# Layer 1's neighbour gather: banded matrices, one shifting transfer per direction, the residual block added on TensorE

## The chip, the cores and the metric

The kernel is one program of four layers on one core of a Trainium2 chip, with TensorE (matrix products), VectorE (DVE), ScalarE (ACT), GpSimd (POOL) and SyncE (SP), which here only starts DMA transfers; sixteen DMA engines serve them. The metric is the device time of one execution in microseconds.

## The reference, cut to what matters

Input is 8 images of 128 channels, 64 x 64 pixels. The change touches layer 1 only. For each pixel it compares the channel vector with its nine neighbours (reflected at the borders), keeps the `kvals` most similar, averages them with exponential weights, adds a group normalisation, and puts a two-layer network behind:

```python
patches = _unfold3x3_reflect(x).reshape(B, C, K2, P)
sim = jnp.einsum('bcp,bckp->bkp', cn, pn)
order = jnp.argsort(-sim, axis=1)
mask = jnp.arange(K2)[None, :, None] < kvals
wts = jnp.exp(top_sim) * mask
wts = wts / jnp.sum(wts, axis=1, keepdims=True)
out = jnp.einsum('bckp,bkp->bcp', pat_sorted, wts).reshape(B, C, H, W)
enhanced = out + _group_norm(x, gn_weight, gn_bias)
h = jax.nn.relu(jnp.einsum('oi,bihw->bohw', w1, enhanced) + b1[None, :, None, None])
ffn = jnp.einsum('oi,bihw->bohw', w2, h) + b2[None, :, None, None]
return enhanced + ffn
```

The program adds the layer's input to this (a residual), and gathers the statistics that the next layer's normalisation needs.

## The kernel before

Images go in pairs, and `layer1` makes `PAIRS + 1` = 5 passes `t` over `STEPS` = 8 steps `c` of `ROWS` = 8 image rows. Pass t works on two things side by side: on pair t the similarities (front half), and on pair t-1 the gather and the network (back half). So pass 0 has a front half only, pass 4 a back half only. Between two passes `weights` turns the sums into weights, 43 us of small VectorE work with a few tiny transfers.

**Front half of a step.** SP loads a block of 512 pixels of both images (`xblk`, L1291). ScalarE normalises it, TensorE transposes it (L1431), and ScalarE copies it to `xt`, in which the partition is the column x of image 0 (0 to 63) or of image 1 (64 to 127) and the free axis holds rows and channels. A neighbour above is then another row in the same partition; a neighbour left or right is another partition. `shift` on SP (L1303 to L1306) makes copies moved by one column, `xleft` and `xright`: for each image and direction one transfer of 63 partitions and one of a single partition, the reflected border, eight per step. Each partition carries 9 x 128 numbers of 4 B. All of them count on the semaphore `shifted[u]`. `shift` waits first until the block is transposed and until the products of two steps before are summed (`summed`), since the copies have two slots. VectorE and GpSimd multiply `xt` with its neighbours (L1674, L1675, L1383, L1389), ScalarE squares, and VectorE sums each product over the channels into `dots` (L1681). At the end of a pass `weights` needs neighbours of `dots` and of the norms `inv_avg`; SP and ScalarE's queue fetch them by twelve small transfers each (L1362, L1619).

**Back half of a step.** TensorE starts two accumulations, one per image, with the group normalisation as a diagonal matrix (L1443). It then adds the neighbours: for each of ten source rows (`SOURCES`), `build` on VectorE (L1641) multiplies three shifted diagonals `diag` (one per dx) with the weights into `wdiag`, and `gather` (L1456) multiplies the source row, as the stationary operand, with them: one product for each dx and image. A source row reaches one, two or three target rows, so a product has 64, 128 or 192 columns. ScalarE moves the sum to `enh` (L1570); TensorE applies the network (`hidden` L1466, `down` L1472); ScalarE moves the result to `res` (L1546); GpSimd adds `enh` (L1397) and then the residual `xres` (L1399); VectorE takes statistics and SP stores. The back half of a step has four 512 KB transfers with the front half's load: `xblk`, `xsum` (for the diagonal), `xres`, and the store.

The order on each engine is written out by hand: every engine has a `step` that calls its parts in a fixed order, and all waits are on semaphores. VectorE's order in a step is builds 0 to 4, side products of the step before, builds 5 and 6, side sums, builds 7 to 9, the other sums, statistics. On SP it is the loads for the next step, `xres`, `shift`, the store of two steps before. A transposing step on TensorE stands behind the first two gathers and one hidden block.

## Time and profile before

| what | value |
|---|---|
| median of 3 runs | 5874.34 us (5872.79 to 5879.55) |
| the profiled execution's own time | 5873.65 us |
| its span, first to last instruction | 5871.9 us |
| layer 1, first block load to last statistics | about 2577 to 3573 us of the span |
| its five passes | 131.6, 174.3, 177.2, 177.8, 163.7 us |
| between the passes | about 43 us each |

The span is the time between the first and the last instruction of the profiled execution, and 1.75 us less than that execution's own time. In the rows below, positions are microseconds from the start of the span. "Busy" of an engine leaves out its register and semaphore work. Names are cut by the profile: `l_prod` is `l1_prod`, and buffer numbers are left out.

### The profile page before, as it was taken

The page shows a single profiled execution, that of the slowest core. Times are in us where ns is not written, and L with a number is a line of the kernel's source. Part 1 is how long each engine was busy: PE and PEld are TensorE (multiplying, and loading weights), DVE is VectorE, ACT ScalarE, POOL GpSimd, SP SyncE. Part 2 cuts the span into 40 slices and gives each one's busy share as a digit, 9 for nine tenths or more (in the row PEclk, how much of TensorE's full clock was granted, in tenths as well). Part 3 has the DMA queues.
Part 4 walks back from the last instruction along what each step waited for, and adds up shares of the span by engine and source line. Part 5 has one row for each costly group of instructions (what it writes and reads, how often), then busy time and mean ns, then how long its engine had stood idle before and what let it go on. Part 6 is the DMA issues. An engine that isn't in the chain of part 4 may idle for free. (4 is left out here: it accounts for less than half of the span.)

```text
span 5871.9 us, 127208 instructions
## 1 busy us (share of the span) xinstructions
PE 4826.6 (82%) x46150; PEld 3795.6 (65%) x46150; DVE 4095.5 (70%) x7785; ACT 3137.9 (53%) x5832; POOL 2837.5 (48%) x2148
## 2 busy tenths in 40 slices
PE   2887878787878787842876875999997999999996
PEld 1655555555656565622544543777777999999996
DVE  5767777776767777767987956999984555555554
ACT  1666666565656566641433424666653544456664
POOL 1535454453535454432543524888882333333364
PEclk9888989898988898965988987999998999999998
DMA  4000000000000000022433421011103000000357
GB/s 146 16 31 16 31 16 31 16 25 22 21 26 17 26 20 16 16 70 91 133 124 102 134 70 53 35 46 41 43 32 134 0 0 0 0 0 0 29 49 151
DMA packets 359128, 268.74 MB, mean 46 GB/s; under 512 B 289440, under 2 KB 290720, under 8 KB 352544
## 3 DMA queue, kind: packets, MB, share of 16 engines
q1 hardware_dynamic: 355264, 258.30, 15.4%
q8 instruction: 275, 4.51, 0.3%
q10 hardware_dynamic: 3424, 4.59, 0.2%
q14 instruction: 165, 1.35, 0.1%
HBM read 156.27 MB, written 67.11 MB: 38 GB/s over the span
## 5 line engine op out<-in xcount | busy, mean ns | idle before, releaser
L527 POOL TENSOR_TENSOR l_probs<-l_probs,l_inv 128x1024 f32<-128x1024 f32 x256 | 492.5, 1929 | 570.3 <-DVE l_inv L937 569.8
L1967 POOL TENSOR_TENSOR l_sum<-l_sum,l_prod 128x1024 f32<-128x1024 f32 x224 | 538.6, 2405 | 111.3 <-ACT l_prod L2064 92.8
L2147 DVE SCALAR_TENSOR_TENSOR l_acc<-l_xpad,l_w,l_acc 128x1024 f32<-128x1024 f32 x448 | 574.5, 1289 | 14.8 <-ACT l_acc L2048 1.3
L606 PEld LDWEIGHTS l_upper<-l_rows_T,l_hats 128*64 128x64 f32 x16384 | 516.1, 142 | 86.8 <-issue 85.0
L773 ACT ACTIVATE l_probs<-l_probs,l_shift 128x256 f32<-128x256 f32 x1024 | 506.9, 496 | 103.6 <-DVE l_shift L922 102.0
L606 PE MATMUL l_upper<-l_rows_T,l_hats 128*64 128x64 f32 x16384 | 551.4, 227 | 0.2 <-issue 0.2
L513 POOL TENSOR_TENSOR l_hats<-l_table,l_place 128x256 f32<-128x256 f32 x256 | 180.4, 705 | 765.4 <-PE l_upper L606 393.2
L590 PE MATMUL l_lower<-l_hats,l_rpe 32*128 32x256 f32 x4096 | 316.1, 425 | 262.6 <-issue 119.7
L517 POOL TENSOR_TENSOR l_hats<-l_table,l_place 128x1024 f32<-128x1024 f32 x256 | 498.7, 1948 | 0.0
L898 DVE TENSOR_SCALAR l_hats<-l_hats 128x1280 f32<-128x1280 f32 x256 | 373.2, 1458 | 168.7 <-ACT l_hats L751 168.5
L2559 DVE TENSOR_TENSOR l_sums_ps<-l_conv_odd,l_even_part 128x256 f32<-128x256 f32 x250 | 108.1, 432 | 453.4 <-PE l_conv_odd L2357 405.5
L922 DVE CUSTOM_DVE_ANT_0 l_probs<-l_lower,l_bias 128x256 f32<-128x256 f32 x1024 | 369.9, 417 | 60.3 <-PE l_lower L621 45.9
L590 PEld LDWEIGHTS l_lower<-l_hats,l_rpe 32*128 32x128 f32 x4096 | 204.3, 197 | 309.8 <-issue 222.9
L634 PEld LDWEIGHTS l_upper<-all_ident,l_probs 128*128 128x128 f32 x2048 | 259.7, 159 | 195.8 <-issue 125.5
L2487 POOL TENSOR_TENSOR l_even_lo<-l_new,l_even_hi 128x256 fp32r<-128x256 f32 x250 | 162.1, 648 | 450.8 <-DVE l_even_hi L2544 450.8
L757 ACT ACTIVATE l_rows_T<-l_lower 128x1024 f32<-128x1024 f32 x256 | 261.4, 1021 | 214.1 <-PE l_lower L590 214.1
L2357 PE MATMUL l_conv_even<-l_even_hi,l_taps 128*128 128x256 f32 x2500 | 357.9, 291 | 15.5 <-DVE l_even_hi L2544 15.2
L621 PE MATMUL l_lower<-l_keys,l_q 32*128 32x256 f32 x2048 | 344.8, 467 | 30.5 <-ACT l_bias L764 15.6
L2357 PE MATMUL l_conv_both<-l_both_hi,l_taps 128*128 128x256 f32 x2500 | 356.6, 290 | 0.0
L634 PE MATMUL l_upper<-all_ident,l_probs 128*128 128x128 f32 x2048 | 328.0, 312 | 29.4 <-POOL l_probs L527 20.9
L751 ACT ACTIVATE l_hats<-l_hats 128x1280 f32<-128x1280 f32 x256 | 323.7, 1265 | 40.2 <-POOL l_hats L517 40.2
L2357 PEld LDWEIGHTS l_conv_even<-l_even_hi,l_taps 128*128 128x128 f32 x2500 | 333.8, 192 | 16.6 <-DVE l_even_hi L2544 16.6
(325 smaller groups left out, 11891.6 us busy)
## 6 DMA issues: line engine op xcount, KB each, us to landing
l_xleft<-l_xt SPq DMA_DIRECT2D x64, 283.5 KB
l_xright<-l_xt SPq DMA_DIRECT2D x64, 283.5 KB
stat_xs<-in_x SPq DMA_DIRECT2D x8, 2048.0 KB, 23.0
l_hats<-in_x SPq DMA_DIRECT2D x8, 2048.0 KB, 7.7
l_xraw<-in_x SPq DMA_DIRECT2D x8, 2048.0 KB, 8.8
after_layer<-l_xraw SPq DMA_DIRECT2D x64, 256.0 KB, 2.0
l_xblk<-after_layer SPq DMA_DIRECT2D x32, 512.0 KB, 5.0
l_xsum<-after_layer SPq DMA_DIRECT2D x32, 512.0 KB, 5.6
```

The lines of the kernel that those rows point to most:

```text
L517: pool.tensor_tensor(xhat(ky).rearrange("c (n i) -> c n i", i=W), grid.rearrange("c (n i) -> c n i", n=1).to_broadcast([C, KW, W]), place[ ...
L527: pool.tensor_tensor(part, part, inv[:, u, cols].rearrange("c (j o) -> c j o", o=1).to_broadcast([C, 4, KEYS]), ALU.mult).then_inc(scaled_ ...
L590: last = pe.matmul(bank[r][:, h * YHAT:(h + 1) * YHAT], rpe[rows, ky // 2, GROUP_HEADS * g + h, :], yhat(ky)[rows, :], start=True, stop=True)
L606: last = pe.matmul(bank[4 + half][64 * s:64 * s + 64, n * UNITS:(n + 1) * UNITS], xhat(ky)[:, k * W:(k + 1) * W], rows_T[:, ky % 2, k, 64 ...
L621: last = pe.matmul(bank[2 * half + h][:, k * KEYS:(k + 1) * KEYS], q[rows, i * C:(i + 1) * C], keys[rows, :], start=True, stop=True)
L634: last = pe.transpose(bank[turned_bank[t]][:, m * C:(m + 1) * C], probs[:, o % 2, 4 * half + m, t * C:(t + 1) * C], sh.ident[:, :])
L773: act.activation(probs[:, u, m, :], probs[:, u, m, :], ACT.Exp, scale=-1.0, bias=shift[:, u, m:m + 1], accum_out=sums[:, u, m:m + 1]).then ...
L898: dve.tensor_scalar(slot, slot, 1.0, 0.0, ALU.subtract, ALU.min).then_inc(hats_ready, 1)
L922: last = dve.tensor_tensor_reduce(probs[:, u, m, :], bank[m // 2][:, (m % 2) * KEYS:(m % 2 + 1) * KEYS], bias[:, unit(o, m), :], 1.0, 3.0e ...
L1967: pool.tensor_tensor(part33(blk), part33(blk), rows(prod33[:, j % PRODUCTS, :]), ALU.add).then_inc(added33, 1)
L2147: last = dve.scalar_tensor_tensor(acc, src, tap, acc, op0=ALU.mult, op1=ALU.add)
L2357: last = pe.matmul(target[:, :, first:first + count], matrix(s, part, kind, j), moving[:, :, at:at + count], start=(p == 0 and q == 0), st ...
```

## The change

- **Banded matrices.** The three diagonals and their products become one band. `band` holds ones on three neighbouring diagonals, 66 columns wide; a source row and target row take 66 numbers of `wband` instead of 3 x 64. The weights are sorted by the residue of the column modulo 3 (`wres`), once per pass, by `by_residue` on VectorE: nine small operations. A gather is then one product for each source row and image, with the same 64, 128 or 192 columns: 20 instead of 60 per step.
- **One shifting transfer per direction.** `xleft[1:128]` comes from `xt` partitions 0 to 126, and `xright[0:127]` from 1 to 127: two transfers of 127 partitions a step instead of eight. The border columns now hold wrong values (a zero, or the other image's column), and the sums made of them are replaced in `dots` before the weights are made, by six two-partition transfers among the twelve on ScalarE's queue. The transfers of `inv_avg` are six instead of twelve. `xleft` and `xright` are zeroed once in the setup.
- **The enhanced block on TensorE.** `down` adds a third product to the accumulation, the identity with `enh`; GpSimd's first addition goes. ScalarE's wait before it writes `enh` again is on `ffn_in_psum` instead of `res_half`.

The diff, cut to its core:

```diff
-        diag = mem.sbuf("diag", [C, 3, W])
-        wdiag = mem.sbuf("wdiag", [C, 9 * ROWS * W])
+        THIRDS = -(-W // 3)
+        BAND = 3 * THIRDS
+        band = mem.sbuf("band", [C, BAND])
+        residue = mem.sbuf("residue", [C, 3])
+        wres = mem.sbuf("wres", [C, H + 2, 3, 3])
+        wband = mem.sbuf("wband", [C, 3 * ROWS * BAND])
...
+            is_third = smem.sbuf("is_third", [C, 3, THIRDS])
...
+                pool.memset(xleft[:, :, :, :], 0.0)
+                pool.memset(xright[:, :, :, :], 0.0)
                 pool.memset(inv_avg[:, :, :, :], 0.0)
                 pool.memset(wsrc[:, :, :, :], 0.0)
-                chain.link(pool.memset(diag[:, :, :], 0.0))
+                pool.memset(band[:, :], 1.0)
+                chain.link(pool.memset(is_third[:, :, :], 0.0))
...
+                    for sign in (-1, 1):
+                        part = band[64 * b:64 * b + 64, :]
+                        chain.link(pool.affine_select(out=part, in_=part, compare_op=ALU.is_ge, fill=0.0, base=1,
+                                                      pattern=[[sign, BAND]], channel_multiplier=-sign))
                     for k in range(3):
-                        part = diag[64 * b:64 * b + 64, k, :]
-                        chain.link(pool.affine_select(out=part, in_=part, compare_op=ALU.not_equal, fill=1.0, base=-(k - 1),
-                                                      pattern=[[-1, W]], channel_multiplier=1))
+                        part = is_third[64 * b:64 * b + 64, k, :]
+                        chain.link(pool.affine_select(out=part, in_=part, compare_op=ALU.not_equal, fill=1.0, base=-k,
+                                                      pattern=[[-3, THIRDS]], channel_multiplier=1))
...
+                dve.reduce_sum(residue[:, :], is_third[:, :, :], axis=LX)
...
-        SHIFTS = 8 * 16
-        NCOLS = 24 * 16
+        SHIFTS = 2 * 16
+        NCOLS = 18 * 16
...
-            start = sum(widths[:s]) * 3 * W
-            return wdiag[:, start:start + widths[s] * 3 * W].rearrange("p (d j x) -> p d j x", d=3, x=W)
+            start = sum(widths[:s]) * BAND
+            return wband[:, start:start + widths[s] * BAND].rearrange("p (j x) -> p j x", x=BAND)
...
-                for b in range(2):
-                    p = 64 * b
-                    sp.dma_start(xleft[p + 1:p + 64, u, :, :], src[p:p + 63]).then_inc(shifted[u], 16)
-                    sp.dma_start(xleft[p:p + 1, u, :, :], src[p + 1:p + 2]).then_inc(shifted[u], 16)
-                    sp.dma_start(xright[p:p + 63, u, :, :], src[p + 1:p + 64]).then_inc(shifted[u], 16)
-                    sp.dma_start(xright[p + 63:p + 64, u, :, :], src[p + 62:p + 63]).then_inc(shifted[u], 16)
+                sp.dma_start(xleft[1:C, u, :, :], src[0:C - 1]).then_inc(shifted[u], 16)
+                sp.dma_start(xright[0:C - 1, u, :, :], src[1:C]).then_inc(shifted[u], 16)
...
+                    at_x = lambda x: slice(x, x + W + 1, W)
+                    moves = [
+                        (inv_avg[at_x(0), 0, 0, 1:H + 1], inv_avg[at_x(1), 0, 1, 1:H + 1]),
+                        (inv_avg[at_x(W - 1), 0, 2, 1:H + 1], inv_avg[at_x(W - 2), 0, 1, 1:H + 1]),
+                    ]
+                    for p in (0, W):
+                        lo, hi = slice(p, p + W - 1), slice(p + 1, p + W)
+                        moves += [(inv_avg[hi, :, 0, 1:H + 1], inv_avg[lo, :, 1, 1:H + 1]),
+                                  (inv_avg[lo, :, 2, 1:H + 1], inv_avg[hi, :, 1, 1:H + 1])]
+                    for to, of in moves:
+                        sp.dma_start(to, of).then_inc(cols_shifted, 16)
...
-                    pool.tensor_tensor(res[:, u, b, :], res[:, u, b, :], enh[:, u, b, :], ALU.add).then_inc(res_half, 1)
-                    pool.wait_ge(res_half, g * 2 + (b + 1))
...
-                    for dx in range(3):
-                        for b in range(2):
-                            at = slice(64 * b, 64 * b + 64)
-                            last = pe.matmul(gather_ps[u][b][:, (s - 2 + first) * W:(s - 1 + final) * W], stage[at, u, s, :],
-                                             matrices(s)[at, dx, :, :].rearrange("p j x -> p (j x)"), start=False,
-                                             stop=(s == SOURCES - 1 and dx == 2))
+                    for b in range(2):
+                        at = slice(64 * b, 64 * b + 64)
+                        last = pe.matmul(gather_ps[u][b][:, (s - 2 + first) * W:(s - 1 + final) * W], stage[at, u, s, :],
+                                         matrices(s)[at, :, 0:W], start=False, stop=(s == SOURCES - 1))
...
-            def down(g, b):
+            def down(g, u, b):
                 wait(pe, ffn_copied, g * 2 + b)
                 for h in range(2):
                     pe.wait_ge(hid_ready, (g * 2 + b) * 2 + (h + 1))
-                    last = pe.matmul(ffn_ps[:, :], w2T[:, h, :], hid[:, b, h, :], start=(h == 0), stop=(h == 1))
-                last.then_inc(ffn_in_psum, 1)
+                    pe.matmul(ffn_ps[:, :], w2T[:, h, :], hid[:, b, h, :], start=(h == 0), stop=False)
+                pe.matmul(ffn_ps[:, :], sh.ident[:, :], enh[:, u, b, :], start=False, stop=True).then_inc(ffn_in_psum, 1)
...
-                wait(act, res_half, (g - 1) * 2)
+                wait(act, ffn_in_psum, (g - 1) * 2)
...
+                    moves = [
+                        (dots[at_x(0), 3, :], dots[at_x(0), 5, :]),
+                        (dots[at_x(0), 0, :], dots[at_x(0), 2, :]),
+                        (dots[at_x(0), 6, 0:H - 1], dots[at_x(1), 0, 1:H]),
+                        (dots[at_x(W - 1), 5, :], dots[at_x(W - 2), 5, :]),
+                        (dots[at_x(W - 1), 2, :], dots[at_x(W - 1), 0, :]),
+                        (dots[at_x(W - 1), 8, 0:H - 1], dots[at_x(W - 2), 2, 1:H]),
+                    ]
+                    for p in (0, W):
+                        lo, hi = slice(p, p + W - 1), slice(p + 1, p + W)
+                        moves += [(dots[hi, 3, :], dots[lo, 5, :]),
+                                  (dots[lo, 8, 0:H - 1], dots[hi, 0, 1:H]),
+                                  (dots[hi, 6, 0:H - 1], dots[lo, 2, 1:H])]
...
-                    dve.tensor_tensor(matrices(s),
-                                      diag[:, :, :].rearrange("p d (o x) -> p d o x", o=1).to_broadcast([C, 3, n, W]),
-                                      wsrc[:, first:final + 1, :, bass.ds(c * ROWS + s, 1)].rearrange("p j d o -> p d j o")
-                                      .to_broadcast([C, 3, n, W]), ALU.mult).then_inc(diag_built, 1)
+                    dve.tensor_tensor(matrices(s).rearrange("p j (m r) -> p j m r", r=3),
+                                      band[:, :].rearrange("p (o m r) -> p o m r", o=1, r=3).to_broadcast([C, n, THIRDS, 3]),
+                                      wres[:, bass.ds(c * ROWS + s, 1), first:final + 1, :].rearrange("p o j r -> p j o r")
+                                      .to_broadcast([C, n, THIRDS, 3]), ALU.mult).then_inc(diag_built, 1)
+
+            def by_residue(t):
+
+                wait(dve, diag_built, (t - 1) * STEPS * SOURCES)
+                for k in range(3):
+                    for r in range(3):
+                        d = (k + 1 - r) % 3
+                        to = wres[:, :, :, r].rearrange("p y j -> p j y")
+                        if k == 0:
+                            last = dve.tensor_scalar(to, wsrc[:, :, d, :], residue[:, k:k + 1], None, ALU.mult)
+                        else:
+                            last = dve.scalar_tensor_tensor(to, wsrc[:, :, d, :], residue[:, k:k + 1], to, op0=ALU.mult, op1=ALU.add)
+                    link(last)
...
+                    by_residue(t)
```

## Rows read from the trace of the kernel before

**Rows 1.** The page: the span, and the shortest landing of a DMA.

```profile
span 5871.9 us, 127208 instructions
...
after_layer<-l_xraw SPq DMA_DIRECT2D x64, 256.0 KB, 2.0
```

**Rows 2.** Busy time in each of the five passes of layer 1.

```profile
core 0: us, PE busy (x) PEld busy (x) DVE busy (x) ACT busy (x) POOL busy (x), PEclk, DMA share, GB/s
2577.00:2708.60 131.60, 17.80 (x64) 11.43 (x64) 91.13 (x65) 29.76 (x42) 47.25 (x16) 0.50 0.37 112
2751.70:2926.00 174.30, 155.48 (x1168) 104.86 (x1168) 158.75 (x159) 74.00 (x104) 91.52 (x44) 0.94 0.45 145
2968.70:3145.90 177.20, 159.55 (x1184) 104.69 (x1184) 163.05 (x163) 77.93 (x110) 97.85 (x48) 0.97 0.46 148
3188.70:3366.50 177.80, 160.44 (x1184) 105.36 (x1184) 162.65 (x162) 77.96 (x110) 102.46 (x48) 0.97 0.45 145
3409.30:3573.00 163.70, 158.27 (x1136) 100.11 (x1136) 73.88 (x102) 55.41 (x77) 48.41 (x36) 0.99 0.24 77
```

**Rows 3.** Time line: first shift issues of two passes, end of the first.

```profile
2585.73 0.95 SPq L1303 DMA_DIRECT2D l_xleft<-l_xt  x1
...
2696.35 2.14 DVE L1674 TENSOR_TENSOR l_prod<-l_xt,l_xleft 128x1024 f32<-128x1024 f32 x1 [1.45 <-DMA l_xright<-l_xt]
...
2708.56 0.19 DVE L1695 COPY l_dots<-l_dots 128x63 f32<-128x63 f32 x1
...
2708.80 9.51 ACTq L1619 DMA_DIRECT2D l_dots<-l_dots  x12
...
2762.58 0.82 SPq L1303 DMA_DIRECT2D l_xleft<-l_xt  x1
```

**Rows 4.** A wait inside the first pass, 2600 to 2700 us.

```profile
DVE l_prod L1674 <- DMA l_xright<-l_xt: 20.8, 4, 7.1
```

**Rows 5.** DMA packets of one step of the first pass, 2614.5 to 2626.9 us.

```profile
DMA packets 689, 1.71 MB, mean 138 GB/s; under 512 B 180, under 2 KB 180, under 8 KB 688
...
q1 hardware_dynamic: 688, 1.70, 44.4%
```

**Rows 6.** Stretches with shift transfers alone; with 2 MB loads alone.

```profile
2598.00:2602.00 4.00, 0.00 (x0) 0.00 (x0) 4.00 (x4) 0.00 (x0) 0.45 (x1) 0.50 0.56 175
2627.50:2634.50 7.00, 0.00 (x0) 0.00 (x0) 7.00 (x5) 0.00 (x0) 1.92 (x1) 0.50 0.54 161
20.00:30.00 10.00, 0.00 (x0) 0.00 (x0) 9.92 (x17) 0.00 (x0) 0.00 (x0) 1.00 1.01 431
```

**Rows 7.** A shift transfer's issue on SP, ns min/median/max.

```profile
L1303 SPq DMA_DIRECT2D l_xleft<-l_xt x64: 757/845/1410, 2585.7 to 3347.4; - x64
```

**Rows 8.** The builds on DVE, all passes, ns min/median/max.

```profile
L1641 DVE TENSOR_TENSOR l_wdiag<-l_diag,l_wsrc x320: 332/744/2908, 2752.1 to 3543.6; 128x576 f32<-128x576 f32 x96, 128x192 f32<-128x192 f32 x32, 128x384 f32<-128x384 f32 x32
```

**Rows 9.** Time line of TensorE, one step of the last pass.

```profile
3429.98 1.98 PE L1443 MATMUL l_gather_ps<-l_xsum,l_gdiag 128*128 128x512 f32 x4
3431.89 1.61 PE L1456 MATMUL l_gather_ps<-l_wdiag,l_stage 64*128 64x64 f32 x24
...
3435.35 3.19 PE L1456 MATMUL l_gather_ps<-l_wdiag,l_stage 64*128 64x192 f32 x36
...
3442.10 2.22 PE L1456 MATMUL l_gather_ps<-l_wdiag,l_stage 64*128 64x192 f32 x24
...
3446.17 2.53 PE L1456 MATMUL l_gather_ps<-l_wdiag,l_stage 64*128 64x192 f32 x36
3448.63 0.70 PE L1443 MATMUL l_gather_ps<-l_xsum,l_gdiag 128*128 128x512 f32 x1
```

**Rows 10.** Time line: a setup memset and two small forms on DVE.

```profile
2567.40 0.60 POOL L1124 MEMSET l_wsrc<- 128x594 f32 x1
...
2743.74 0.42 DVE L1760 SCALAR_TENSOR_TENSOR l_sim<-l_sim,l_edge 128x192 f32<-128x192 f32 x1
2744.19 0.35 DVE L1761 TENSOR_SCALAR l_sim<-l_sim,l_edge 128x192 f32<-128x192 f32 x1
```

More of the change, by code:

```diff
@@ L1348, in _ @@
                     sp.wait_ge(cols_ready, t + 1)
-                    for b in range(2):
-                        p = 64 * b
-                        lo, hi = slice(p, p + 63), slice(p + 1, p + 64)
-                        first, second, but1, last = (slice(p + q, p + q + 1) for q in (0, 1, 62, 63))
-                        moves = [
-                            (inv_avg[hi, 0, 0, 1:H + 1], inv_avg[lo, 0, 1, 1:H + 1]),
-                            (inv_avg[hi, 1, 0, 1:H + 1], inv_avg[lo, 1, 1, 1:H + 1]),
-                            (inv_avg[lo, 0, 2, 1:H + 1], inv_avg[hi, 0, 1, 1:H + 1]),
-                            (inv_avg[lo, 1, 2, 1:H + 1], inv_avg[hi, 1, 1, 1:H + 1]),
-                            (inv_avg[first, 0, 0, 1:H + 1], inv_avg[second, 0, 1, 1:H + 1]),
-                            (inv_avg[last, 0, 2, 1:H + 1], inv_avg[but1, 0, 1, 1:H + 1]),
-                        ]
-                        for to, of in moves:
-                            sp.dma_start(to, of).then_inc(cols_shifted, 16)
+                    at_x = lambda x: slice(x, x + W + 1, W)
[9 more added lines that the diff above has]
+                        sp.dma_start(to, of).then_inc(cols_shifted, 16)
                     sp.wait_ge(weights_ready, t + 1)
@@ L1488, in step @@
                     if before:
-                        down(g, 0)
+                        down(g, 1 - u, 0)
                         hidden(g, 1 - u, 1)
@@ L1493, in step @@
                     if before:
-                        down(g, 1)
+                        down(g, 1 - u, 1)
                     if t >= 1:
@@ L1507, in _ @@
                 hidden(g, 1, b)
-                down(g, b)
+                down(g, 1, b)
         @block.scalar
@@ L1605, in _ @@
                     act.wait_ge(summed, (t + 1) * STEPS)
-                    for b in range(2):
-                        p = 64 * b
-                        lo, hi = slice(p, p + 63), slice(p + 1, p + 64)
-                        first, second, but1, last = (slice(p + q, p + q + 1) for q in (0, 1, 62, 63))
-                        moves = [
-                            (dots[hi, 3, :], dots[lo, 5, :]),
-                            (dots[first, 3, :], dots[first, 5, :]),
-                            (dots[lo, 8, 0:H - 1], dots[hi, 0, 1:H]),
-                            (dots[last, 8, 0:H - 1], dots[but1, 2, 1:H]),
-                            (dots[hi, 6, 0:H - 1], dots[lo, 2, 1:H]),
-                            (dots[first, 6, 0:H - 1], dots[second, 0, 1:H]),
-                        ]
-                        for to, of in moves:
-                            act.dma_start(to, of).then_inc(cols_shifted, 16)
+                    at_x = lambda x: slice(x, x + W + 1, W)
+                    moves = [
[11 more added lines that the diff above has]
+                                  (dots[hi, 6, 0:H - 1], dots[lo, 2, 1:H])]
+                    for to, of in moves:
+                        act.dma_start(to, of).then_inc(cols_shifted, 16)
                     act.wait_ge(sims_ready, t + 1)
```

2 lines of the change are left out of this document (removed).

## The prediction

> **What bounds the kernel now.** The change lies in layer 1 alone, so I read the page for the span, 5871.9 us [rows 1], then busy time by pass. Layer 1 makes five passes over eight steps each: pass 0 computes neighbour sums only, passes 1 to 3 those of one pair of images and the output of the pair before, pass 4 output only. They last 131.6, 174.3, 177.2, 177.8 and 163.7 us [rows 2], with some 43 us of weight arithmetic after each of the first four. What limits them differs. In passes 1 to 3 VectorE is busy 159 of 174 us and TensorE 155, both nearly full. In pass 4 TensorE is busy 158 of 164. In pass 0 neither is: VectorE 91 of 131.6, with TensorE at its 1.2 GHz level (granted 0.50) [rows 2]. The wait view says what VectorE lacks there: in 100 us it idles 20.8 us before the first side product, for the right shifting transfer [rows 4]. So SBUF-to-SBUF transfers already end last in pass 0, with eight transfers a step in place. That sent me to the DMA views.
>
> **How those transfers run.** One step of pass 0 issues four transfers of 63 rows, four of one row and one 512 KB load. The queue counts 688 packets, 180 of them under 512 B [rows 5]. A row is 4608 B (9 x 128 x 4). Four times 63 rows are 252 packets; a single row went as 16 packets of 288 B, so 64; the load is 256 packets of 2 KB. That leaves 116 tiny ones, and 116 = 4 x 9 + 5 x 16: one completion from each of nine engines for a 63-row transfer, from each of sixteen for the others. With sixteen everywhere the sum would be 716 and 208. The share agrees: while shifts run alone, 0.56 and 0.54 of the sixteen engines are busy [rows 6], and 9/16 is 0.5625. So a transfer's rows are not dealt out freely: 63 rows = 9 engines x 7, 128 rows = 16 x 8. Both are what comes out if the engine count is the largest number up to 16 that divides the rows.
>
> **The shifting transfers of the change.** Per direction there is now one transfer of 127 rows. 127 is prime. By the pattern just read the count is 1, and 585,216 B go through one engine; two directions make 1.170 MB a step. The trace has no one-engine transfer of this size, so its pace is bounded by two rows. Below: nine engines with the same packets move 161 GB/s at share 0.54, 161/(0.54 x 16) = 18.6 GB/s each [rows 6]. Above: sixteen engines with whole-image loads move 431 GB/s, 26.9 each [rows 6]. I take 25.5, near the upper row, since the nine read and write the same half of the partitions at the same time and a lone engine has no such company. That is 1.170 MB / 25.5 GB/s = 45.9 us a step (43.5 to 62.9), against a whole step now of about 131.6/8 = 16 us in pass 0 and 176/8 = 22 us in passes 1 to 3.
>
> The same engine also carries its sixteenth of each 512 KB transfer, 32.8 KB or 1.3 us: one in a step of pass 0, four (block, sum and residual loads, store) in passes 1 to 3. Both directions must share an engine for this sum; had they two, it is the second rival. A step then takes S0 = 45.9 + 1.3 = 47.2 us (44.7 to 64.7) in pass 0 and S1 = 45.9 + 5.2 = 51.1 us (48.4 to 69.9) in passes 1 to 3.
>
> The Trainium skill says the same outright, and names this very case: in "DMA: Bandwidth & Descriptors", section "Why a DMA increments its semaphore by 16 and not by 1", a DMA issued from SP or ACT uses the largest count up to 16 that divides the slowest dimension of both patterns, 127 partitions get 1, and it is always the lowest-numbered engines that are taken. The completions counted above bear out the rule at 63 and 128 rows; no row here shows it at 127, nor which engine is taken. By its last part both directions queue on one engine. Its rule for authors (one transfer rather than two halves) speaks for the change, this rule against it, and by this rule the sum is the one above.
>
> **Does the engine stay busy?** Shift c is issued by SP once step c is turned and the products of step c-2 are summed. Those products wait for shift c-2. From its landing VectorE needs about 12.2 us (2696.35 to 2708.56) [rows 3], and the turn behind TensorE's first gathers and hidden block about 10 us more at the low clock. Meanwhile shift c-1 runs for 47 us or more. So the next is always queued in time, the engine never idles, and steps cost exactly S. The same slack hides everything else in passes 0 to 3, where compute needs 22 us of a 47 to 51 us step. SP is in order: behind a late shift wait the store of step c-2 and the next block, sum and residual loads, all of them needed one step later only.
>
> **Sum of the passes.** Pass 0: first issue to last column now takes 2708.56 - 2585.73 = 122.8 us [rows 3]; then 8 x 47.2 + 2.0 (a landing, [rows 1]) + 12.2 = 391.8, so +269. Passes 1 to 3: first issue 10.9 us after the pass begins (2751.7 to 2762.58) [rows 2, 3], about 2 us more with the new vector step below, then 8 x 51.1 + 2.0 + 12.2: 435.9 each, 1307.7 in all against 529.3 now [rows 2], so +778.
>
> **Builds.** 10 a step; one of 192, 384 or 576 elements takes 332 to 744 ns undisturbed (median 744 for the widest) [rows 8], so 0.126 us plus 1.07 ns an element. With 66, 132 and 198 elements they cost 2 x 0.20 + 2 x 0.27 + 6 x 0.34 = 3.0 us in place of 6.2. In passes 1 to 3 this is worth nothing: the transfer covers it. Without that cover it is in the first rival.
>
> **Gathers and identity.** A TensorE step of pass 4 runs from 3429.98 to 3448.63, 18.65 us; its gathers take 1.61 + 3.19 + 2.22 + 2.53 = 9.55 us [rows 9]. Two in three go: -6.4. The identity adds one 128x512 product per image; a group of two products takes 1.98 us with its tail, about 0.86 each [rows 9]: +1.7. So -4.7 a step, -37 us in pass 4, nothing in passes 1 to 3. If ScalarE's hand-overs end last instead, a part stays away: -20 to -37, I take -37. POOL loses one of two additions; it is on no path except the last microseconds.
>
> **New work by residue.** Nine VectorE forms of 198 elements ahead of each of passes 1 to 4: like 0.35 and 0.42 us for 192 elements [rows 10], 3 x 0.35 + 6 x 0.42 = 3.6 us, on the path. For passes 1 to 3 it is in the 2 us above (quicker first builds give back 1.6); pass 4 +3.6.
>
> **Setup.** Two memsets of 2304 elements; 594 elements took 0.60 us [rows 10], so 2 x 2.3 or less, say 4, and 1 for four selects: +5 (0 if weight loads hide it).
>
> **Edges.** inv_avg goes by 6 transfers, not 12, dots still by 12 on ACT's queue, and that chain, 9.51 us of issues [rows 3], ends last: 0 (-4 to +1 over all four).
>
> Total: 5873.65 (the profiled execution's own time; its span is 5871.9 and the median of the runs 5874.34, so no correction) + 269 + 778 - 37 + 4 + 5 = **6893 us**. At 26.9 GB/s the steps lose 2.5 x 8 + 2.7 x 24 = 85 us: 6808. At 18.6 they gain 17.5 x 8 + 18.8 x 24 = 591: 7484.
>
> **Rivals.** (1) *Faster: the rows are dealt out unevenly over most engines.* If 127 rows go as eight to an engine, transfers end no later than now and SP issues two instead of eight (0.85 us the larger, [rows 7]). Then TensorE sets passes 1 to 3, 155.5/8 = 19.4 - 4.7 = 14.7 us a step, VectorE with POOL beside it about as much; say 15.5 against 20.8: -127 us over 24 steps. Pass 4 gives -37, pass 0 about -15 of its waits, new work +19: 5714 us (5690 to 5790). It decides from the point where a shift transfer lands within some 15 us; for that 127 rows must get five engines or more. Against it: 63 rows would then have got more than nine.
> (2) *Two engines.* Each direction gets one engine, but not the same. The step falls by half of 45.9: 6893 - 32 x 22.95 = 6159 us. Against it: nothing shows transfers of one queue taking turns among engines, but nothing excludes it either.
> (3) *Nothing moves:* gains and a partly slower transfer cancel. It needs a pace in a narrow band.
>
> **Chances.** Forecast 0.87, rival 1 0.08, rival 2 0.04, rival 3 0.01. Range 6800 to 7490: the forecast's own, with both ends of the pace; it leaves out 0.13. A run of this kernel can tell a difference of about 0.2%, 12 us. Faster 0.08, same 0.01, slower 0.91.
>
> **What the profile after would show.** DMA share near 1/16 = 0.06 through pass 0, at 23 to 27 GB/s; steps of 47 and 51 us; VectorE waiting 30 us a step on xleft or xright; TensorE at its low level in passes 0 to 3; a packet count of 254 rows a step with 2 completions; pass 4 near 130 us. Wrong if the share stays above 0.3 in pass 0 (rival 1), or is 0.12 (rival 2). Steps of 60 us and more would mean the pace was mis-sized, gaps in the DMA row between steps that SP's waits are late.

## The result, and the profile after

The changed kernel takes **6848.09 us** (median of four runs, 6846.43 to 6849.19) beside 5874.9 us for the kernel before on the same chip: ratio 1.1655 with a 95% interval of 1.1635 to 1.1675. It is slower by a sixth, in the way that was forecast; the forecast was 6893 us, the range 6800 to 7490.

The page, its span line, its busy line, and the group of the first side product (busy us, mean ns, then the idle time of VectorE just before it and what ended most of it).

```profile
span 6845.7 us, 122063 instructions
...
PE 4785.2 (70%) x43718; PEld 3675.8 (54%) x43718; DVE 4004.6 (58%) x7822; ACT 3130.8 (46%) x5832; POOL 2721.0 (40%) x2091
...
L1690 DVE TENSOR_TENSOR l_prod<-l_xt,l_xleft 128x1024 f32<-128x1024 f32 x32 | 83.6, 2612 | 1137.6 <-DMA l_xright<-l_xt 922.8
```

VectorE idles 1137.6 us in all ahead of 32 side products. In the kernel before it was 72.2 us, so this wait alone grew by 1065 us, more than the loss of 973 us (6848 - 5875):

```profile
L1674 DVE TENSOR_TENSOR l_prod<-l_xt,l_xleft 128x1024 f32<-128x1024 f32 x32 | 51.6, 1613 | 72.2 <-DMA l_xright<-l_xt 61.0 <-issue 10.4 <-DVE l_dots L1681 0.5
```

The busy times by pass (columns as in [rows 2], which they answer):

```profile
2579.00:2967.20 388.20, 17.80 (x64) 11.43 (x64) 90.11 (x65) 29.76 (x42) 40.73 (x16) 0.50 0.10 38
3012.90:3432.30 419.40, 150.49 (x556) 77.86 (x556) 133.92 (x159) 72.35 (x104) 65.84 (x30) 0.64 0.16 57
3477.20:3900.20 423.00, 159.12 (x576) 79.95 (x576) 137.67 (x162) 75.80 (x110) 68.28 (x32) 0.66 0.17 58
3945.20:4367.00 421.80, 155.83 (x576) 78.43 (x576) 137.32 (x163) 75.78 (x110) 68.28 (x32) 0.67 0.16 57
4411.90:4545.40 133.50, 129.32 (x532) 62.05 (x532) 42.19 (x102) 54.63 (x77) 23.55 (x18) 0.98 0.27 85
```

Pass 0 went from 131.6 to 388.2 us, passes 1 to 3 from some 176 to some 421, with none of the compute engines busy for even half of them; pass 4, which has no shifting transfers, fell from 163.7 to 133.5. The DMA view of one step of pass 0, 2636.5 to 2682 us (40 slices, GB/s in each), against [rows 5, 6]:

```profile
DMA  0000000000000000000000000003930000000000
GB/s 25 28 24 28 24 28 28 24 28 24 28 24 28 24 28 24 28 24 28 24 28 24 28 28 24 28 24 75 312 118 28 24 28 24 28 24 28 28 24 25
DMA packets 524, 1.69 MB, mean 37 GB/s; under 512 B 18, under 2 KB 18, under 8 KB 524
...
l_xblk<-after_layer SPq DMA_DIRECT2D x1, 512.0 KB, 37.5
```

The GB/s row never falls below 24 and never rises above 28 but for the one 512 KB load in the middle: one engine, always busy. 18 small packets are 16 completions of that load and one for each direction's shift. A step of pass 2, 3587.1 to 3637.9 us, has no gap either, and four transfers of 512 KB in it:

```profile
GB/s 26 26 26 27 25 25 29 25 25 25 29 38 25 29 25 25 29 25 25 25 29 25 25 29 25 25 25 103 330 33 176 255 53 278 121 148 278 33 25 26
```

The time line of VectorE in pass 0, and of SP's issues in a step of pass 1:

```profile
2636.28 3.39 DVE L1690 TENSOR_TENSOR l_prod<-l_xt,l_xleft 128x1024 f32<-128x1024 f32 x1 [57.26 <-DMA l_xright<-l_xt]
...
2682.22 3.33 DVE L1690 TENSOR_TENSOR l_prod<-l_xt,l_xleft 128x1024 f32<-128x1024 f32 x1 [34.65 <-DMA l_xright<-l_xt]
```

```profile
3166.15 15.38 SPq L1314 DMA_DIRECT2D l_xright<-l_xt  x1
3181.57 22.04 SPq L1333 DMA_DIRECT2D after_layer<-l_res  x1
3203.73 2.66 SPq L1303 DMA_DIRECT2D l_xblk<-after_layer  x1
3206.44 3.29 SPq L1328 DMA_DIRECT2D l_xsum<-after_layer  x1
3209.77 0.47 SPq L1321 DMA_DIRECT2D l_xres<-after_layer  x1
3210.35 7.17 SPq L1313 DMA_DIRECT2D l_xleft<-l_xt  x1
3217.56 15.75 SPq L1314 DMA_DIRECT2D l_xright<-l_xt  x1
```

A step of pass 0 is 45.9 us (2682.22 - 2636.28), one of passes 1 to 3 is 50.8. The issues are the surprise: an issue of a shift took 0.8 to 1.4 us before [rows 7], and now 15 us for the right shift and 22 for the store. The likely reading is that the queue to the one engine is full and the sequencer stands in the issue until there is room; no view shows the queue itself.

### The profile page after: what moved, and what is told of

Same layout as the page of the kernel before. It is cut to its first block and busy times, and to the rows that moved or that the text cites. A ratio compares the mean times of both kernels' runs of the same rounds, so it can differ in the third digit from the quotient of the medians.

```text
span 6845.7 us, 122063 instructions
## 1 busy us (share of the span) xinstructions
PE 4785.2 (70%) x43718; PEld 3675.8 (54%) x43718; DVE 4004.6 (58%) x7822; ACT 3130.8 (46%) x5832; POOL 2721.0 (40%) x2091
## 5 line engine op out<-in xcount | busy, mean ns | idle before, releaser
L1690 DVE TENSOR_TENSOR l_prod<-l_xt,l_xleft 128x1024 f32<-128x1024 f32 x32 | 83.6, 2612 | 1137.6 <-DMA l_xright<-l_xt 922.8
L1458 PE MATMUL l_gather_ps<-l_wband,l_stage 64*128 64x192 f32 (+2 forms) x1280 | 150.7, 371 | 631.4 <-DVE l_wband L1644 631.4
L606 PEld LDWEIGHTS l_upper<-l_rows_T,l_hats 128*64 128x64 f32 x16384 | 515.7, 142 | 86.5 <-issue 84.7
L1394 POOL TENSOR_TENSOR l_prod<-l_xt,l_xright 128x1024 f32<-128x1024 f32 x32 | 86.5, 2704 | 1094.6 <-DMA l_xright<-l_xt 1094.6
L1458 PEld LDWEIGHTS l_gather_ps<-l_wband,l_stage 64*128 64x128 f32 x1280 | 114.9, 220 | 722.0 <-DVE l_wband L1644 664.9
L1547 ACT ACTIVATE l_res<-l_ffn_ps,l_b 128x512 f32<-128x512 f32 x64 | 44.0, 687 | 861.8 <-DMA after_layer<-l_res 538.8
L2374 PE MATMUL l_conv_even<-l_even_hi,l_taps 128*128 128x256 f32 x2500 | 357.4, 290 | 15.7 <-DVE l_even_hi L2561 15.4
```

Of the source, the lines that this page charges most:

```text
L606: last = pe.matmul(bank[4 + half][64 * s:64 * s + 64, n * UNITS:(n + 1) * UNITS], xhat(ky)[:, k * W:(k + 1) * W], rows_T[:, ky % 2, k, 64 ...
L1458: last = pe.matmul(gather_ps[u][b][:, (s - 2 + first) * W:(s - 1 + final) * W], stage[at, u, s, :], matrices(s)[at, :, 0:W], start=False, ...
L2374: last = pe.matmul(target[:, :, first:first + count], matrix(s, part, kind, j), moving[:, :, at:at + count], start=(p == 0 and q == 0), st ...
```

## The experiments

Unless told otherwise each is timed against the kernel before on the same chip; a step is the distance between two starts of the first side product, a pass runs from the scaled identity (gdiag) to the last column.

**Was it the transfers alone?** The changed kernel with the eight old transfers:

```
-                sp.dma_start(xleft[1:C, u, :, :], src[0:C - 1]).then_inc(shifted[u], 16)
-                sp.dma_start(xright[0:C - 1, u, :, :], src[1:C]).then_inc(shifted[u], 16)
+                for b in range(2):
+                    p = 64 * b
+                    sp.dma_start(xleft[p + 1:p + 64, u, :, :], src[p:p + 63]).then_inc(shifted[u], 16)
+                    sp.dma_start(xleft[p:p + 1, u, :, :], src[p + 1:p + 2]).then_inc(shifted[u], 16)
...
-        SHIFTS = 2 * 16
+        SHIFTS = 8 * 16
```

> The changed kernel with the old eight shifting transfers of a step (63 rows and 1 row for each image and direction); banded matrices, edge mending, identity and the rest stay. Theory (one engine carries all 127 rows of both directions): all of the loss goes and the rest of the change shows its own worth, about 5720 us (5690 to 5790), DMA share in pass 0 back near 0.37. Rival (the slowdown comes from another part: the builds or gathers waiting, the mended edges, the identity): stays above 5875 us, near 6848.

Measured: 5790.41 us, ratio 0.9854 (0.9837 to 0.9870). So two lines of the change make 1058 us of loss (6848 - 5790), and the rest of it is a gain of some 86. That gain is less than was expected of it (5720 us): passes 1 to 3 come down to 148, 159 and 156 us, where eight steps of 15.5 us would be 124.

**What sets the number of engines?** The same kernel with each direction in two parts, once 112 + 15 rows, once 125 + 2 (there the pairs are 0, 125 and 125, 127):

```
+                for lo, hi in ((0, 112), (112, 127)):
+                    sp.dma_start(xleft[lo + 1:hi + 1, u, :, :], src[lo:hi]).then_inc(shifted[u], 16)
+                    sp.dma_start(xright[lo:hi, u, :, :], src[lo + 1:hi + 1]).then_inc(shifted[u], 16)
```

> The changed kernel with each direction cut in two: 112 rows and 15 rows, four transfers a step; both numbers have a divisor of 14 to 16. Theory (the count of engines is the largest number up to 16 that divides the rows): 16 and 15 engines, so at most 8 rows of a direction on one engine, no limit left, 5700 us (5670 to 5780), at or a little below the kernel with eight transfers since SP issues half as many. Rival (a transfer that spans both images' halves, or more than 64 partitions, or the shared semaphore, is what is slow): 112 rows span both halves too, so it stays near 6848.

> Each direction as 125 rows and 2 rows. Theory: 125 rows go on 5 engines, 25 rows each; the fullest engine carries about 52 rows a step, 52 x 0.175 = 9.1 us and up to 5 us of the other loads, 14 us: just under the step that compute sets, so 5720 to 5800 us with a DMA share near 5/16 while shifts run. Rival (rows are dealt unevenly, or the count has nothing to do with divisors): 125 and 127 rows differ by 2 per cent, near 6830.

Measured: 5750.23 us (0.9786, 0.9769 to 0.9802) with 112 + 15, and 5839.09 us (0.9938, 0.9921 to 0.9955) with 125 + 2. Same bytes, same number of transfers, 89 us apart. A stretch of pass 0 with nothing but rows of the 125 + 2 transfers in flight (columns as in [rows 2]: the last two are DMA share and GB/s), one with nothing but those of 112 + 15, and two landings of the latter:

```profile
2622.00:2624.00 2.00, 0.00 (x0) 0.00 (x0) 2.00 (x2) 0.00 (x0) 0.00 (x0) 0.50 0.32 92
...
2617.00:2619.00 2.00, 0.00 (x0) 0.00 (x0) 2.00 (x3) 0.00 (x0) 0.00 (x0) 0.50 0.98 267
```

```profile
l_xleft<-l_xt SPq DMA_DIRECT2D x1, 504.0 KB, 4.0
l_xright<-l_xt SPq DMA_DIRECT2D x1, 504.0 KB, 4.8
```

0.32 of sixteen is five engines, and 5 is the largest divisor of 125 up to 16. 112 = 16 x 7 goes over all, a share of 0.98: such a transfer lands in 4 to 5 us, where a 127-row pair takes 44. The share of 9/16 for 63 rows [rows 6] and of 1/16 for 127 are the other two points of the same pattern. The Trainium skill, "DMA: Bandwidth & Descriptors", section "Why a DMA increments its semaphore by 16 and not by 1", states this as its rule, and the runs agree at 63, 112, 125 and 127 rows.

**Do both directions really queue on one engine?** First one direction alone in one piece, the other as before (four transfers):

```
                 sp.dma_start(xleft[1:C, u, :, :], src[0:C - 1]).then_inc(shifted[u], 16)
-                sp.dma_start(xright[0:C - 1, u, :, :], src[1:C]).then_inc(shifted[u], 16)
+                for b in range(2):
+                    p = 64 * b
+                    sp.dma_start(xright[p:p + 63, u, :, :], src[p + 1:p + 64]).then_inc(shifted[u], 16)
+                    sp.dma_start(xright[p + 63:p + 64, u, :, :], src[p + 62:p + 63]).then_inc(shifted[u], 16)
```

> Left as one transfer of 127 rows, right as the old four. Theory (both directions queue on the same engine): the one engine carries 127 rows instead of 254, and the nine-engine transfers add 14 to it, 141 x 0.175 = 24.7 us; steps of 26 us in pass 0 and 30 us in passes 1 to 3 instead of 45.7 and 49.6, so 6848 - 8 x 20 - 24 x 20 = 6210 us (6150 to 6300). Rival (the two directions were on two engines side by side, each at half the pace): one direction alone still takes its 45 us, near 6848.

Measured: 6234.21 us (one run). Steps are 26 to 27 us in pass 0 and 30 to 32 after it: of the 254 rows of a step the engine still carries 127 and one in nine of the 126 that go in 63-row transfers, so 141, and a step of pass 0 falls from 45.8 to some 27 us. One direction alone doesn't take its old 45 us.

Then the right shift moved to ScalarE's queue, right behind its copies of the turned block, where the old wait for the summed products is met:

```
-                sp.dma_start(xright[0:C - 1, u, :, :], src[1:C]).then_inc(shifted[u], 16)
...
+                        act.wait_ge(turn_copied, (n + 1) * 2)
...
+                        act.dma_start(xright[0:C - 1, u, :, :], rows_of(t, c * ROWS, ROWS + 1)[1:C]).then_inc(shifted[u], 16)
```

> The changed kernel, but the right shifting transfer (127 rows) is issued by ScalarE's queue, right behind the turned copies, the left one still by SP's. Theory A (every one-engine transfer goes to the same engine, whatever queue issues it): steps stay 45.8 and 50.8 us, DMA share 0.06, 6848 us (6820 to 6900). Theory B (each queue deals from an engine of its own): two engines at once, steps near 24 and 28 us, DMA share 0.12, 6848 - 32 x 22.9 = 6115 us (6080 to 6200).

Measured: 6834.29 us (one run), theory A. With nothing but the two queues' shifts in flight:

```profile
2600.00:2630.00 30.00, 0.00 (x0) 0.00 (x0) 0.00 (x0) 0.00 (x0) 0.00 (x0) 0.50 0.06 26
...
2597.23 18.16 SPq L1313 DMA_DIRECT2D l_xleft<-l_xt  x1
2597.23 0.65 ACTq L1595 DMA_DIRECT2D l_xright<-l_xt  x1
...
2615.84 42.08 SPq L1303 DMA_DIRECT2D l_xblk<-after_layer  x1
```

A share of 0.06 and 26 GB/s from two queues is still one engine. A second queue doesn't bring a second engine; SP waits even longer, 42 us, in the issue of a load. ScalarE doesn't: its issue at 2597.23 us, to the same engine and at the same moment as one of SP's that takes 18.16 us, is over in 0.65, and the median of its 32 is 0.65 too (9.3 the longest). So what is held up is the queue that has the backlog, and not every issuer.

**Two engines.** Cut at 122 = 2 x 61:

```
+                for lo, hi in ((0, 122), (122, 127)):
```

> The changed kernel with each direction cut into 122 and 5 rows. If the engine count is the largest number up to 16 that divides the rows, 122 rows (2 x 61) go over two engines and 5 rows over five: the two busiest engines carry 61 + 1 rows of each direction, a step of (2 x 62 x 4608 B)/26.4 GB/s = 21.6 us and 1.3 more in pass 0, 5.2 in passes 1 to 3: 23 and 27 us. Then 6848 - 32 x 23.5 = 6096 us (6060 to 6150). If rows were dealt by size or evenly: 5750 as with 112 rows.

Measured: 6140.93 us (one run), 45 us above the estimate but nowhere near the 5750 of 112 rows. The share with shifts alone is that of two engines:

```profile
2604.00:2608.00 4.00, 0.00 (x0) 0.00 (x0) 0.00 (x0) 0.00 (x0) 0.00 (x0) 0.50 0.13 53
```

Steps are 23.4 us in pass 0 (23 expected) and 29.0 in the middle of passes 1 to 3 (27 expected). Of the 2 us, some 1.6 are a term that was mis-sized (4 x 0.4, next section); the rest isn't explained.

**Does the engine hide all the rest?** The kernel before with only the transfers of the change, its moves of dots and inv_avg and its two memsets; diag, wdiag, three products a source and POOL's two additions stay:

```
+                sp.dma_start(xleft[1:C, u, :, :], src[0:C - 1]).then_inc(shifted[u], 16)
+                sp.dma_start(xright[0:C - 1, u, :, :], src[1:C]).then_inc(shifted[u], 16)
```

> The kernel before, with only the two 127-row transfers (and the edges mended in the dots); three products per gather, wide matrices and POOL's two additions stay. Theory (in passes 0 to 3 the one DMA engine sets the step and hides all compute): steps of 45.8 and 50.8 us as in the changed kernel, so the same time but for pass 4, which stays at some 164 us from its scale (+30), and without the four by_residue of 4.05 us (-16): 6862 us (6845 to 6885). Rival (the longer builds and gathers still count behind a late transfer): a step longer by some of the 3.2 us of builds, up to +77 us more, 6900 to 6940.

Measured: 6861.01 us, ratio 1.1678 (1.1658 to 1.1697). Its middle steps, 45.6 to 45.9 and 50.4 to 51.2 us, are those of the changed kernel although TensorE makes three times the gather products and VectorE's builds are longer. In passes 1 to 3 those parts are worth nothing beside this transfer (1263 us in all against 1264). Its pass 2, then pass 4 (as in [rows 2]; 423.0 and 133.5 us in the changed kernel):

```profile
3465.20:3888.20 423.00, 180.09 (x1184) 119.53 (x1184) 169.26 (x163) 76.81 (x110) 93.01 (x48) 0.72 0.17 62
4392.10:4556.60 164.50, 159.09 (x1136) 100.56 (x1136) 73.92 (x102) 55.43 (x77) 48.44 (x36) 0.98 0.24 77
```

**What are the other parts worth?** Each alone on the kernel before. The bands (with by_residue), then the identity, then the transfers cut at 112:

```
-                    for dx in range(3):
-                        for b in range(2):
...
+                    for b in range(2):
...
+                                         matrices(s)[at, :, 0:W], start=False, stop=(s == SOURCES - 1))
```

> The kernel before, with only the banded matrices (one product per source and image, by_residue); eight shifting transfers, POOL's two additions. If the gain of the eight-transfer run (0.985) is the gathers' 6.4 us a step on TensorE and the builds' 3.2 on VectorE, it is nearly all here or more, since the identity costs TensorE 1.7 us a step: pass 4 -40, passes 1 to 3 -60, by_residue +16: 5785 us (5765 to 5810). Rival (the second addition on POOL is what holds VectorE and ScalarE's hand-overs, so the gathers' saving is not used without the identity): 5830 or more.

```
-                    pool.tensor_tensor(res[:, u, b, :], res[:, u, b, :], enh[:, u, b, :], ALU.add).then_inc(res_half, 1)
+                pe.matmul(ffn_ps[:, :], sh.ident[:, :], enh[:, u, b, :], start=False, stop=True).then_inc(ffn_in_psum, 1)
```

> The kernel before, with only the enhanced block added by TensorE's identity. Theory (TensorE is near full in passes 1 to 4, and two more products a step lie on it): +1.7 us a step in pass 4 (+14), passes 1 to 3 0 to +1.7 a step: 5895 us (5875 to 5930), slower. Rival (POOL's addition held up VectorE or the block's end): faster, 5840 to 5870.

```
-                for b in range(2):
...
+                for lo, hi in ((0, 112), (112, 127)):
```

> The kernel before, with only the shifts as four transfers of 112 and 15 rows over 16 and 15 engines and mended edges. Theory (in passes 1 to 3 compute sets 21 us of the step, the transfers only part of its waits): pass 0 -12, passes 1 to 3 -10, setup +5: 5857 us (5835 to 5875). Rival (transfers over nine engines already set the steps of passes 1 to 3 of the kernel before): -25 or more from passes 1 to 3 as between the two runs with bands and identity, 5830 or less.

Measured: bands 5796.35 us (0.9863, 0.9847 to 0.9880); identity 5919.87 us (1.0070, 1.0053 to 1.0087); transfers 5841.21 us (0.9940, 0.9923 to 0.9956). Pass 2 of the three, then pass 4 of bands alone, of bands with identity (the run with eight transfers), and of identity alone:

```profile
2958.10:3121.00 162.90, 124.10 (x544) 62.96 (x544) 134.36 (x162) 76.90 (x110) 84.70 (x48) 0.89 0.47 152
...
2975.40:3168.10 192.70, 176.28 (x1216) 112.58 (x1216) 151.67 (x163) 77.94 (x110) 74.00 (x32) 0.96 0.43 136
...
2946.90:3120.60 173.70, 159.43 (x1184) 104.67 (x1184) 159.73 (x163) 77.97 (x110) 107.07 (x48) 0.98 0.48 151
...
3376.50:3495.00 118.50, 112.94 (x496) 54.60 (x496) 49.45 (x103) 54.68 (x77) 46.85 (x36) 0.98 0.30 96
...
3355.40:3489.20 133.80, 129.60 (x532) 62.07 (x532) 42.21 (x102) 54.64 (x77) 23.54 (x18) 0.98 0.26 85
...
3446.20:3624.10 177.90, 173.70 (x1172) 106.94 (x1172) 65.30 (x102) 55.42 (x77) 22.84 (x18) 0.99 0.22 71
```

The bands give 82 us, nearly all of the gain. The identity alone **costs** 42 us: TensorE is nearly full in the kernel before, as VectorE is, and in pass 2 it is now busy 176 us against 160 [rows 2]. On top of the bands it neither gains nor loses (0.9863 and 0.9854, with intervals that overlap; the run with both also has the mended edges, some 7 us less, and the two memsets, some 4 more), but not evenly: passes 1 to 3 last 463 us in all with it and 481 without, while pass 4, where POOL has no products to make and its additions are free, is 133.8 us with it and 118.5 without. The cut at 112 rows is worth 37 us by itself and 40 on top of the other two; most of it falls in pass 0 (106.8 us from the first shift to the last column, against 122.8) and 11 us in passes 1 to 3, so transfers over nine engines didn't set the steps there. On top of the other two, where the steps are shorter, passes 1 to 3 get 26 of the 40 us (463 to 437).

**A version that beats both.** With 112 + 15 rows; the scaled identities before the wait for the shifted weights, and POOL's two memsets moved from ahead of its masks to behind them:

```
+                pool.sem_inc(masks_ready, 1)
+                pool.memset(xleft[:, :, :, :], 0.0)
+                pool.memset(xright[:, :, :, :], 0.0)
...
+                    scales(t)
+                    dve.wait_ge(weights_shifted, WS * t)
+                    by_residue(t)
```

> The version with 112 and 15 rows (5750 us), with the scaled identities built before the wait for the shifted weights and by_residue behind them, and POOL's two memsets of the shifted buffers issued after its masks, where they hold up nobody. If by_residue and the memsets lie on the path: four times 4 us and 4.6 us less, 5730 us (5722 to 5740). Rival (VectorE's first builds of a pass wait for by_residue anyway and the pass starts with them): only the memsets, 5746.

Measured: 5738.02 us (0.9767, 0.9751 to 0.9783): 12 us of the 20. Setup is shorter by 2.1 us only: the first block load is issued 12.4 us after the layer's first transfer, 14.5 with the memsets ahead and 9.9 in the kernel before, so moving them gives back half of that 4.6 us. The rest is theirs too, for the most part: the run with bands and no memsets has 10.6, those with the new transfers and memsets but no bands 13.4. Why they still cost behind the masks isn't shown. And from the last vector form of the weights to the first side product of pass 2 the gain is 1.8 us, not 4. What became of the rest is in TensorE's rows around the start of that pass, first in this version, then in the one with 112 + 15 alone (windows as in [rows 2], where the value ahead of the last two is the granted clock, then the first gathers and the hidden block's products):

```profile
2914.00:2918.00 4.00, 3.75 (x4) 1.17 (x4) 0.00 (x0) 0.00 (x0) 0.00 (x0) 0.50 0.24 50
2918.00:2922.90 4.90, 0.00 (x0) 0.00 (x0) 4.34 (x11) 0.00 (x0) 0.00 (x0) 0.50 0.93 321
...
2922.98 1.23 PE L1459 MATMUL l_gather_ps<-l_wband,l_stage 64*128 64x64 f32 x8 [5.15 <-DVE l_wband L1645]
2924.14 3.40 PE L1468 MATMUL l_hid_ps<-l_enh,l_w1T 128*128 128x512 f32 x4
```

```profile
2931.40:2934.00 2.60, 2.60 (x14) 1.45 (x14) 0.53 (x2) 0.69 (x1) 0.00 (x0) 1.00 0.00 0
...
2931.43 0.72 PE L1459 MATMUL l_gather_ps<-l_wband,l_stage 64*128 64x64 f32 x8
2932.07 1.98 PE L1468 MATMUL l_hid_ps<-l_enh,l_w1T 128*128 128x512 f32 x4
```

Last, the same with the blocks of the last pair of images added by POOL, those of the first three by the identity:

```
+                if not last_pair:
+                    last = pe.matmul(ffn_ps[:, :], sh.ident[:, :], enh[:, u, b, :], start=False, stop=True)
...
+                    if last_pair:
+                        pool.tensor_tensor(res[:, u, b, :], res[:, u, b, :], enh[:, u, b, :], ALU.add).then_inc(res_half, 1)
```

> The version with 112 and 15 rows and the earlier scales (5738 us), but the blocks of the last pair are added by GpSimd as in the kernel before, those of the first three pairs by TensorE's identity. From the traces: with bands alone pass 4 takes 118.5 us from its scale to its last statistic, with bands and identity 133.8; in passes 1 to 3 the identity saves some 18 us in all. If the identity's cost in pass 4 is TensorE's (GpSimd has no products there): -15 us, 5723 us (5717 to 5730). Rival (the saving of the run with bands alone is its shorter hand-overs in another order, or the tail's second addition takes it back): 5735 or more.

Measured: **5725.63 us** (0.9742, 0.9729 to 0.9755), 12 us less again, all of it in pass 4, which takes 127.7 us from its scales where the version ahead took 139.9. This is 152 us better than the kernel before and 1122 better than the change.

## Why the prediction was right, step by step

**The engine count** held: 127 rows on one engine, both directions on the same. It came from the packets and shares of 63 rows [rows 5, 6], and the runs with 112, 122, 125 and 127 rows show it (shares 0.98, 0.13, 0.32 and 0.06).

**The pace** was a choice, 25.5 GB/s between 18.6 and 26.9. A step of passes 1 to 3 is 50.8 - 45.8 = 5.0 us longer than one of pass 0 and moves three more 512 KB transfers: by this subtraction 1.7 us for each one's sixteenth, where 1.3 was reckoned. That leaves 45.8 - 1.7 = 44.1 us for 1.170 MB, 26.5 GB/s. The upper row was the right neighbour. The trace doesn't show why a load costs 1.7 us: 32.8 KB in that time would be 20 GB/s. The two errors offset, which is luck: steps 45.8 and 50.8 against 47.2 and 51.1.

**The sum.** Pass 0 came 13 us under its term (first issue 2588.33, last column 2967.23: 378.9 us against 391.8). Passes 1 to 3, each from its first by_residue form to its last column, last 423, 427 and 426 us against 435.9: 31 under, more than the steps explain: first and last steps of a pass are shorter than 51 (47 to 50), presumably because not all of the 512 KB transfers fall into them. Pass 4 is 163.8 - 133.5 = 30 us shorter, not 37: a TensorE step takes 14.68 us (4444.31 to 4458.99), not 13.95. The identity's term holds (1.7 us a step; 133.8 against 118.5 us, above, makes 1.9). The gathers' was mis-sized, answering [rows 9]:

```profile
4446.22 0.71 PE L1458 MATMUL l_gather_ps<-l_wband,l_stage 64*128 64x64 f32 x8
...
4448.78 1.25 PE L1458 MATMUL l_gather_ps<-l_wband,l_stage 64*128 64x192 f32 x12
...
4454.45 0.92 PE L1458 MATMUL l_gather_ps<-l_wband,l_stage 64*128 64x192 f32 x8
...
4458.07 0.99 PE L1458 MATMUL l_gather_ps<-l_wband,l_stage 64*128 64x192 f32 x12
```

A third of the products takes 0.71 + 1.25 + 0.92 + 0.99 = 3.87 us, more than a third of 9.55: 5.7 us go, not 6.4. by_residue is 4.05 us against 3.6, setup +4.6 against +5. The first gap between last column and gdiag is 45.7 us against 43.1, the other three 44.9 against 42.8, with by_residue's 4.05 in each: the edges gave 1.5 to 2.0 us each time, 7 in all, where 0 was taken from a range down to -4. Together -13 - 31 + 7 - 7 is -44, and 6893 - 44 = 6849 against 6848 measured. So part of the closeness is offsetting errors; the mechanism and its main term held.

**Does the engine stay busy** held in its result and missed in its reason. SP's queue was to be ahead by a margin; instead SP is stuck in the issues of right shifts and stores (medians 15.7 and 21.8 us), and ScalarE waits 538.8 us from 2800 to 4400 us for stores of results, which land 38.8 us after their issue (median), 2.7 at best. None of this costs, since the DMA rows shown have no gap. In the run with two queues, the steps of passes 1 to 3 swing between 62 and 38 us and their mean stays.

**TensorE at its low level** was right for pass 0 (0.50) and too strong for passes 1 to 3: there the mean is 0.64 to 0.67. In one step of pass 2 it is 1.00 from 3562 to 3567 us, at the end of the step's products, and 0.50 from 3572 to 3587, in the wait.

**The first rival** had a threshold that the runs don't contradict and too large a gain. Five engines are enough to beat the kernel before (0.9938 with 125 + 2 rows), two are not (6141 us); three and four weren't tried. With sixteen, 5750 us came in place of 5714: the term that failed is the step of passes 1 to 3, 15.5 us assumed and 17.1 measured in passes 2 and 3 (16.1 in pass 1). The three passes came down from 529 to 437 us, 92 in place of the 127 forecast. TensorE's 14.7 us is met, but VectorE, reckoned at "about as much", needs more:

```profile
2927.30:3075.50 148.20, 129.41 (x576) 64.71 (x576) 126.68 (x163) 75.51 (x110) 65.49 (x32) 0.96 0.53 166
```

VectorE is busy 127 of 148 us, TensorE 129, and each hands over to the other several times a step. The builds were priced at 3.0 us a step from undisturbed rows; here they take 5.4 (192 of 602 ns on average, 64 of 608 and 64 of 272, together 172 us over 32 steps), because single ones stretch where POOL makes its products:

```profile
2945.83 0.63 DVE L1645 TENSOR_TENSOR l_wband<-l_band,l_wres 128x198 f32<-128x198 f32 x2
...
2949.87 2.49 POOL L1395 TENSOR_TENSOR l_prod<-l_xt,l_xright 128x1024 f32<-128x1024 f32 x1
2950.07 2.44 DVE L1645 TENSOR_TENSOR l_wband<-l_band,l_wres 128x132 f32<-128x132 f32 x1
```

Two builds of 198 elements take 0.63 us together; one of 132, begun beside POOL's product, takes 2.44 and ends with it (the shortest of that size is 0.28). That this stretch is what keeps the step at 17 us was not tried by itself.

**The second rival** was priced well (6159 against 6141 for two engines) and its condition is false: neither two transfers of one queue nor two queues take turns among engines.

## What to carry to other kernels

Count the partitions of a transfer before you merge transfers: what matters is the largest divisor up to 16 of the row count, and 127 rows, a prime number above 16, put all of it on one engine, the same one for both directions and both queues tried. Cut an awkward count into a multiple of 16 and a rest (112 + 15, not 127, not 63 + 1). And price an operation that is moved to another engine per stage: with the bands in place the same identity product costs 15 us where GpSimd has nothing else to do, and saves 18 where it has; without them it costs in every pass.

## What the runs showed of the hardware

- **A backlog on one DMA engine holds up the issuer whose queue has it.** SP's issues that took 0.4 to 1.4 us took 15 to 22 us, 42 at most (with two queues feeding the engine), also those of 512 KB transfers that are spread over all engines. ScalarE's issues to the same engine took 0.65 us (median) meanwhile. That a sequencer with other work behind such issues would lose the time is an inference: SP has none.
- **A merged transfer is not the better one by itself.** The Trainium skill, "DMA: Bandwidth & Descriptors", section "Rules for kernel authors", says of two transfers to disjoint partition halves not to bother and to use one of 128 partitions, since both spread over all engines anyway. Here the measurement decides otherwise off the round numbers: one of 127 rows is slower than two of 63 rows and two single ones by 1058 us in this kernel, and 112 + 15 is better than both. Its remark that queues of several issuers end on the same engines is borne out by the run with two queues.
- **VectorE and POOL slow one another.** Their side products are released together, and the one that starts second ends as if it had waited for the other. In 21 of the 32 steps of the changed kernel POOL's starts first: it takes 2.34 us and VectorE's 3.04 to 3.41. In the other 11 VectorE's starts first: it takes 1.23 us and POOL's 3.39 to 3.42. VectorE's second product, with nothing beside it, takes 1.21. Its sums over one block don't stretch: in the run with 112 + 15 rows one takes 1.21 us right beside POOL's product (2947.51 and 2947.55).

```profile
2636.25 2.34 POOL L1394 TENSOR_TENSOR l_prod<-l_xt,l_xright 128x1024 f32<-128x1024 f32 x1 [45.53 <-DMA l_xright<-l_xt]
2636.28 3.39 DVE L1690 TENSOR_TENSOR l_prod<-l_xt,l_xleft 128x1024 f32<-128x1024 f32 x1 [57.26 <-DMA l_xright<-l_xt]
2639.60 1.21 DVE L1691 TENSOR_TENSOR l_prod<-l_xt,l_xright 128x1024 f32<-128x1024 f32 x1
```

What stays open: why each 512 KB transfer adds 1.7 us to the one engine, the last half microsecond of the 29.0 us steps with 122 + 5 rows, and by which hand-over the identity saves 18 us in passes 1 to 3 on top of the bands (POOL's busy time falls from 84.7 to 70.1 us a pass there, but VectorE's doesn't fall with it).
